# A four-branch graph network on one core: the sum carried from one tile of edges to the next leaves the products as a column and is added by VectorE, instead of being a row of the product's input

## The reference

```
edge_index = jnp.stack([src, dst])
h = jnp.maximum(_layernorm(x), 0.0);  x = x + gcn(h, edge_index, ...)     # 512 -> 128 -> 512
h = jnp.maximum(_layernorm(x), 0.0);  x = x + sage(h, src, dst, ...)      # three layers, below
h = jnp.maximum(_layernorm(x), 0.0);  x = x + edges(h, edge_index, ...)   # messages, below
h = jnp.maximum(_layernorm(x), 0.0);  x = x + last(h, edge_index, ...)    # mean, two products, batch norm

# sage, for l in range(3):
h_neigh = jax.ops.segment_sum(h[src], dst, num_segments=n) / deg
rst = jax.nn.relu(h @ W_self[l] + h_neigh @ W_neigh[l] + b[l])
h = rst / jnp.maximum(jnp.sqrt(jnp.sum(rst * rst, axis=-1, keepdims=True)), EPS)

# edges:
hidden = mish(concat([h[src], h[dst], edge_attr]) @ W1 + b1)
messages = mish(hidden @ W2 + b2)
agg = jax.ops.segment_sum(messages, dst, num_segments=n)
u = mish(concat([h, agg]) @ W3 + b3);  out = layernorm(h + u @ W4 + b4)
```

## Time and profile before

| | |
|---|---|
| timed, median of 3 runs | 3239.72 us (3235.13 to 3242.54) |
| the profiled execution's own time | 3228.05 us |
| its span | 3226.3 us |
| PE busy (matmuls) | 2661.2 us, 82% |
| DVE / ACT / POOL busy | 1783.5 / 1490.4 / 1351.1 us |
| mean granted clock of PE | 0.949 |
| SP's DMA queue | 359870 packets, 369.76 MB |

### The profile page before, as it was taken

The page is one execution under the profiler, slowest core; times in us unless marked ns, Lnnn a source line. Parts: engine busy times, 40 slices in busy tenths (PEclk is TensorE's granted clock), DMA queues, the critical chain, the costliest instruction groups (busy, mean ns, idle before and its releaser), DMA issues. The chain is left out here.

```text
span 3226.3 us, 47724 instructions
## 1 busy us (share of the span) xinstructions
PE 2661.2 (82%) x13893; PEld 1437.7 (45%) x13893; DVE 1783.5 (55%) x3993; ACT 1490.4 (46%) x2158; POOL 1351.1 (42%) x2421
## 2 busy tenths in 40 slices
PE   0025669778797999799996988979999999899976
PEld 0025533333343444344453545655555555444444
DVE  7625657656764874489764443425555556423234
ACT  3216746433432442245432774546666666432152
POOL 3664568858632332156543541113333333300136
PEclk9999988989999999999997998999999999999985
DMA  5418956646744784466644322222222233300148
GB/s 166 147 50 256 289 178 213 198 131 154 181 121 128 181 197 116 128 209 218 200 143 149 92 84 79 67 81 99 98 98 98 98 118 131 119 1 22 48 167 349
DMA packets 390005, 451.65 MB, mean 140 GB/s; under 512 B 202419, under 2 KB 228388, under 8 KB 387165
## 3 DMA queue, kind: packets, MB, share of 16 engines
q1 hardware_dynamic: 359870, 369.76, 37.0%
q0 software_dynamic: 29984, 80.02, 8.5%
HBM read 190.68 MB, written 217.75 MB: 127 GB/s over the span
## 5 line engine op out<-in xcount | busy, mean ns | idle before, releaser
L217 PE MATMUL s_ps_z<-s_w,slots 128*128 128x512 f16 x2844 | 647.8, 383 | 64.7 <-DMA s_bias<-in_L_gnn_b 43.1
L217 PEld LDWEIGHTS s_ps_z<-s_w,slots 128*128 128x128 f16 (+1 forms) x2844 | 277.7, 99 | 391.6 <-issue 48.2
L1352 ACT ACTIVATE s_g<-s_g,s_rn 128x512 f32<-128x512 f32 x237 | 170.3, 718 | 304.2 <-POOL s_rn L1231 304.0
L2019 PE MATMUL u_ps_o<-u_w,u_uT 128*128 128x512 f32 x632 | 288.5, 599 | 0.3 <-DVE u_uT L1890 0.3
L1281 DVE SCALAR_TENSOR_TENSOR s_g<-s_ps_z,s_f,s_bias 128x512 f32<-128x512 f32 x237 | 177.4, 748 | 195.2 <-PE s_ps_z L217 186.0
L1231 POOL TENSOR_TENSOR s_rn<-s_em,minus_half 128x1 f32<-128x1 f32 x237 | 171.9, 726 | 212.5 <-DVE s_em L1296 206.5
L2001 PE MATMUL u_ps_z<-slots,u_w 128*128 (+2 forms) x1920 | 236.1, 273 | 0.0
L2127 PE MATMUL z_ps_z<-slots,z_w 128*128 128x512 f16 (+1 forms) x960 | 210.1, 378 | 7.2 <-DMA z_w<-split_root 7.2
L2001 PEld LDWEIGHTS u_ps_z<-slots,u_w 128*128 128x128 f16 x1920 | 173.5, 98 | 37.5 <-issue 0.4
L707 DVE BATCH_NORM_STATS2 u_ny_st<-u_ps_o 128x6 f32<-128x512 f32 x79 | 54.7, 693 | 212.7 <-PE u_ps_o L2019 212.7
L734 ACT ACTIVATE u_h<-u_x,u_n_sh,u_n_rs 128x512 f32<-128x512 f32 x79 | 64.2, 813 | 229.2 <-POOL u_n_sh L729 229.2
(11 more groups left out here) (362 smaller groups left out, 5652.5 us busy)
## 6 DMA issues: line engine op xcount, KB each, us to landing
h_rows<-s_g SPq DMA_DIRECT2D x158, 256.0 KB, 2.3
x_rows<-r_x SPq DMA_DIRECT2D x79, 256.0 KB, 2.9
s_x<-x_rows SPq DMA_DIRECT2D x79, 256.0 KB, 2.9
x_rows<-s_x SPq DMA_DIRECT2D x79, 256.0 KB, 2.0
h_rows<-s_h SPq DMA_DIRECT2D x79, 256.0 KB, 2.4
u_x<-x_rows SPq DMA_DIRECT2D x79, 256.0 KB, 2.9
x_rows<-u_x SPq DMA_DIRECT2D x79, 256.0 KB, 2.1
h_rows<-u_h SPq DMA_DIRECT2D x79, 256.0 KB, 2.3
```

The lines of the kernel that those rows point to most:

```text
L217: ins = nc.tensor.matmul(out_ap, a(c), w[:, part * size + c * n:part * size + (c + 1) * n], start=first and c == 0 and m == 0, stop=stop a ...
L1352: nc.scalar.activation(g[b][:, :], g[b][:, :], ACT.Relu, scale=rn[v.buf(2)][:, 0:1]).then_inc(s_h, 1)
L2019: ins = nc.tensor.matmul(ps_o[b][:, :], ut_tile(v, c), w4[:, c * D:(c + 1) * D], start=False, stop=c == C - 1)
```

## The change

The carry's product and the carry row are gone. Columns of the selections `RAW` and `MEAN` that were for row 0 (column 0) now hold the selection of the carry, so the sums' own product gives, as column 0 of each feature chunk, what goes on to the next tile. Row 0 of `sl` is zero in SBUF, and only rows 1 to 127 are fetched. What row 0 of the selection did is done by VectorE in float32: row 0 is fetched a second time, spread to all 128 partitions (`w0`), and `total = w0 * on + ps_a` is formed for each chunk, where `on` is column 0 of the tile before. `total` is written over `m`, so `m` is free only when `lo` is done, not when the product is done. `hi` and `lo` read `total`, columns 1 to 127. `batch_rows` has one buffer for `sl` and `w0` (`nsel=1`). In `sage_layer` the unused output of `length` goes to PSUM (in `ps_c`'s place) as float32. In `prepare` PE makes the carry column three times. `unscale` is made in `node_update` by DVE.

```diff
+    class Carry:
+        def load(self, sp, t, kind):
+            b = t.buf(self.n)
+            wait_count(sp, self.s_added, t.t + 1 - self.n)
+            sp.dma_start(self.w0[b][:, :],
+                         sel_d[0:1, bass.ds(t.t * SELW + kind * P, P)].to_broadcast([P, P])).then_inc(self.w0_in[b], 16)
...
+        def add(self, dve, t, ps_a, total):
+            b, w0 = t.buf(2), t.buf(self.n)
+            dve.wait_ge(self.w0_in[w0], 16 * (t.uses(self.n) + 1))
+            wait_count(dve, self.s_on, t.t)
+            for c in range(C):
+                ins = nc.vector.scalar_tensor_tensor(out=total[:, c, :], in0=self.w0[w0][:, :],
+                                                     scalar=self.on[1 - b][:, c:c + 1], in1=ps_a[:, c * P:(c + 1) * P],
+                                                     op0=MUL, op1=ADD)
+            ins.then_inc(self.s_added, 1)
+            dve.wait_ge(self.s_added, t.t + 1)
+            nc.vector.tensor_copy(self.on[b][:, :], total[:, :, 0]).then_inc(self.s_on, 1)
...
         def load(self, sp, e):
-            wait_count(sp, self.s_sum, e.t - 1)
-            sp.dma_start(self.sl[e.buf(2)][:, :],
-                         sel_d[:, e.t * SELW + self.kind * P:e.t * SELW + (self.kind + 1) * P]).then_inc(
-                self.sel_in[e.buf(2)], 16)
+            b = e.buf(self.nsel)
...
+            wait_count(sp, self.s_sum, e.t + 1 - self.nsel)
+            sp.dma_start(self.sl[b][1:P, :],
+                         sel_d[1:P, e.t * SELW + self.kind * P:e.t * SELW + (self.kind + 1) * P]).then_inc(
+                self.sel_in[b], 16)
+            self.carry.load(sp, e, self.kind)
...
         def gather(self, pool, e):
             b = e.buf(self.nm)
-            wait_count(pool, self.s_sum, e.t + 1 - self.nm)
+            wait_count(pool, self.s_lo, e.t + 1 - self.nm)
...
         def sums(self, pe, e):
             b = e.buf(self.nm)
-            pe.wait_ge(self.s_carried, e.t + 1)
-            nc.tensor.matmul(self.ps_c[0:1, :], carry_c[:, e.t:e.t + 1], self.m[b][:, :], start=True,
-                             stop=True).then_inc(self.s_carry, 1)
...
-            wait_count(pe, self.s_lo, e.t)
...
+            wait_count(pe, self.carry.s_added, e.t)
             for c in range(C):
                 ins = nc.tensor.matmul(self.ps_a[:, c * P:(c + 1) * P], self.m[b][:, c * P:(c + 1) * P],
-                                       self.sl[e.buf(2)][:, :], start=True, stop=True)
+                                       self.sl[e.buf(self.nsel)][:, :], start=True, stop=True)
...
-                    pipeline(dve, NT, (FT - 2, edge_carry), (0, z_sum), (0, length), (0, clamp), (2, lo_rows),
+                    pipeline(dve, NT, (0, z_sum), (FT - 2, edge_add), (0, length), (0, clamp), (2, lo_rows),
                              (FT - 2, edge_lo), (FT - 3, edge_moments), edges=edges, loop_end=LOOP_END)
...
                     for c in range(C):
-                        if c < len(edges_of(g + 1)):
-                            sums.carry(dve, edges_of(g + 1)[c])
                         if 0 < c <= len(edges_of(g + 1)):
-                            sums.lo(dve, edges_of(g + 1)[c - 1])
+                            sums.add(dve, edges_of(g + 1)[c - 1])
                         dve.wait_ge(s_z, C * g + c + 1)
...
+                        if 0 < c <= len(edges_of(g + 1)):
+                            sums.lo(dve, edges_of(g + 1)[c - 1])
                     if len(edges_of(g + 1)) == C:
+                        sums.add(dve, edges_of(g + 1)[C - 1])
                         sums.lo(dve, edges_of(g + 1)[C - 1])
```

More of the change, by code:

```diff
@@ L185, in gnn_program @@
     floor_col = sb(top, "floor_col", [P, 1])
-    unscale = sb(top, "unscale", [P, P], F16)
     slots16 = slots[:, :].bitcast(F16)
@@ L1041, in __init__ @@
             self.m = [sb(ctx, f"{phase}_m{b}", [P, D]) for b in range(nm)]
[L1042 to L1045, removed]
+            self.sl = [sb(ctx, f"{phase}_sel{b}", [P, P]) for b in range(nsel)]
+            self.s_sum, self.s_hi, self.s_lo = sems(phase, "sum ahi alo")
@@ L1046, in __init__ @@
+            self.m_in, self.sel_in = pair(phase, "min", nm), pair(phase, "selin", nsel)
+            self.carry = Carry(ctx, f"{phase}_carry", nsel)
             self.norm = Norm(ctx, f"{phase}_en", 2) if normed else None
@@ L1148, in halves @@
                 return tuple(t[:, k * D:(k + 1) * D].rearrange("p (c n) -> p c n", c=C) for k in range(2))
-            sums = EdgeSums(ctx, phase, h_d[l] if l else x1_d, MEAN, scale_in, 2, halves, ps_a, ps_c, normed=l == 0)
+            sums = EdgeSums(ctx, phase, h_d[l] if l else x1_d, MEAN, scale_in, 2, halves, ps_a, normed=l == 0)
             s_inv, s_slot, s_slot_i = sems(phase, "inv slot sloti")
@@ L1159, in edge_gather, with edge_add @@
                 sums.gather(nc.gpsimd, e)
-            def edge_carry(e):
-                sums.carry(nc.vector, e)
+            def edge_add(e):
+                sums.add(nc.vector, e)
             def edge_lo(e):
@@ L1270, in _ @@
                 dve.wait_ge(s_f, 1)
+                sums.clear(nc.vector, *(t[:, :] for t in aT))
                 dve.wait_ge(s_w, 32)
@@ L1637, in _ @@
                 dve.wait_ge(s_f, 1)
+                passed.clear(dve, *(t[0:1, :] for t in sl), *(t[:, :] for t in aT))
                 def z_sum(v):
@@ L1647, in cap, with add @@
                     mish.cap(dve, r[:, :], v, s_sum, v.t - 1)
-                def carry(v):
-                    dve.wait_ge(mish.s_u, v.t + 1)
-                    if isinstance(v.t, int) and v.t == 0:
-                        nc.vector.memset(mish.c[v.buf(2)][0:1, :], 0.0).then_inc(s_carried, 1)
-                        return
-                    dve.wait_ge(s_carry, v.t)
-                    nc.vector.tensor_copy(mish.c[v.buf(2)][0:1, :], ps_c[0:1, :]).then_inc(s_carried, 1)
+                def add(v):
+                    dve.wait_ge(s_sum, v.t + 1)
+                    wait_count(dve, s_aT, v.t)
+                    passed.add(dve, v, ps_a[v.buf(2)], total[:, :].rearrange("p (c n) -> p c n", c=C))
                 def totals(v):
@@ L1753, in node_update @@
             minus_f = sb(ctx, "u_minus_f", [P, 1])
+            unscale = sb(ctx, "u_unscale", [P, P], F16)
             uT = [sb(ctx, f"u_uT{b}", [P, C * 2 * P]) for b in range(2)]
@@ L1867, in _ @@
                 dve.wait_ge(s_w, 96)
+                nc.vector.tensor_scalar(out=unscale[:, :], in0=ident[:, :], scalar1=1.0 / SCALE_LN, scalar2=None, op0=MUL)
                 nc.vector.tensor_scalar(out=w4[:, :], in0=w4[:, :], scalar1=f[:, 0:1], scalar2=None,
@@ L2085, in _ @@
                                         scalar2=None, op0=MUL).then_inc(s_f, 1)
+                sums.clear(dve, *(t[:, :] for t in aT))
                 for g in range(GROUPS):
```

102 lines of the change are left out of this document (57 added, 45 removed).

## The result

The changed kernel takes 3409.39 us (median of 4 runs, 3405.21 to 3413.42), the one before, run beside it, 3241.13: a ratio of 1.0522 (1.0501 to 1.0542), +168 us. The prediction said slower, 3364 (3300 to 3415): the direction and the range hold, and the loss is 44 us larger than its +124. The profiled execution took 3405.21, its span is 3403.2.

A forecast was written before the change was run, and what follows sets the result against it. PE was taken to bound layer 0, `edge_messages` and `batch_rows`. Terms 58.9 + 79.8 + 17.5 − 8 − 16.4 − 8.6 + 1 = +124.2 us on the profiled 3228.05 gave 3352.3, on the median 3364 (3300 to 3415).

The forecast's parts named there:

- The loop: Layers 0 and 1: adds awaiting sums delay the next `sl` fetch; steps 10.3 and 11.4 us, +58.9 and +79.8.
- S+5.27: Layers 0 and 1: the next `sl` fetch is issued 5.27 us after S, the start of a tile's sums.
- The 127 rows: Fetch of `sl`: 127 rows go through one DMA engine, 2.8 us more on the landing.
- The clock: Layers 0 and 1: idle PE drops its clock, half of 38 sums take 0.92 us longer, +17.5.
- Layer 2: Layer 2: `sl` landing, 7.1 us against 6.4 in hand, eats most of PE's 0.95 a step; −8 us.
- batch_rows: `batch_rows`: −19 us from PE, +5.8 at group boundaries, +4.6 in the last group; together −8.6.
- edge_messages: `edge_messages`: bound by PE, −19 us, less two open tails of adds at 1.3 each; −16.4.
- the PE term of 0.95 a step: Carry products gone from PE: −0.95 us x 20 in each zone that PE bounds.
- Rival 1: Fetch of 127 rows spreads over 16 engines, landings stay 2.2 and 3.3 us: 3208 to 3228, say 3222; chance 0.13.
- Rival 2: The second fetch, `w0`, comes last; each us late costs 38, so 3402 for one; chance 0.06.
- The PSUM term (+1): `length` output to PSUM: +1 us, bounds 0 to 14.

The follow-up runs named there:

- experiment 5: Changed kernel with 13 (layer 0) or 18 (layer 1) unread PE products ahead of each sums: 3358.61 us against 3220.55 for the kernel before.
- experiment 3: Changed kernel with VectorE's adds moved behind `lo_rows`, 127 rows kept: 3270.3 us against 3241.03 for the kernel before.
- experiment 4: Changed kernel with the two fetches first in SyncE's list, 127 rows and early adds kept: 3193.28 us against 3241.03 for the kernel before.
- experiment 1: Kernel before with only rows 1 to 127 of `sl` fetched, nothing else moved: 3277.88 us against 3241.03.
- experiment 2: Changed kernel with `sl` fetched as 128 rows and `w0` in its own DRAM tensor: 3255.21 us against 3241.03 for the kernel before.
- experiment 9: Changed kernel with only 122 rows of `sl` fetched (6 to 127): 3279.1 us against 3221.85 for the kernel before.
- experiment 6: Changed kernel with the two fetches first in SyncE's list and layer 0's moments ahead of `lo`: 3184.56 us against 3220.55 for the kernel before.
- experiment 8: Changed kernel with 128 rows, fetches first in SyncE's list and layer 0's moments behind the adds: 3149.41 us against 3220.55 for the kernel before.

## Why the prediction was right, and where its sizes were off

*The loop* is shown, link by link, and it is what the forecast of +124 rests on. At the full clock the changed kernel issues the fetch at S+5.27 (the two full-clock steps of layer 0, and the median of 30 steps of experiment 5): the prediction's figure to the hundredth, which is part luck, since single links were off by up to 0.06 and cancelled. At the low clock it is S+6.19, the 0.92 more of the sums. Experiments 3 and 4 cut the loop at two different links, and both take away most of the loss.

*The 127 rows* are shown by experiments 1, 2 and 9. The term was 2.8 us; with and without, the landings differ by at least 3.2 in layer 0 and by 2.8 in layer 1. But I had added it to medians of the kernel before: 5.0 and 6.1 became 5.49 and 6.57, 0.5 more in each of 38 steps, 18 us.

*The clock* was, for its size, mis-sized most. I let half of the 38 sums be low, because a low step leaves less idle. In the changed kernel 15 of 20 were in layer 0 and all 20 in layer 1. Over the 38 steps the issue of the fetch came 29.4 us later than S+5.27 would give, not 17.5: 12 of the missing 44. What failed was "that step's idle is only 2 to 3 us, and the next may run at full clock". The idle behind a low step had a median of 3.3 us in layer 0 and 4.1 in layer 1. And 2 to 3 us did not keep the clock up either: idles of 2.5 (experiment 2) and 2.2 (experiment 5) were followed by low sums. Experiment 5, with 6 low sums of 40, brings the 29.4 down to 7.

*The first fetch of a zone* had no term in the sum. PE already waited for it in layer 1 of before (5.13 idle), so a longer landing counts in full. From the start of a layer's projection to its first sums it took 3.9 and 3.2 us more in layers 0 and 1, and +0.5 and −0.9 in experiment 2 with its 128 rows. That is 7 us. The tails of the two zones, where the last adds lie open, are another 4. With the 18 and the 12 these make 41 of the 44; what is left lies within the differences of the other stages.

*Layer 2* came out near (−11 for −8) by a wrong mechanism, that is by luck. I had `sl` late; it is the gather that is late, landing in 6.8 instead of 4.9 beside the 127 rows. With 128 rows it lands in 4.6 and the step is 6.5.

*`batch_rows`*: −3.9 for −8.6. There too the sums wait for the gather, 0.3 to 0.8 us in 8 of 20 tiles. It may now go out only after `lo`, since the totals are written over `m`; the prediction named that wait for layer 0 alone. With 128 rows the stage takes 296, so 8 of the 12 us that it could win are lost to the row count. `edge_messages` (−18.6 for −16.4) and the PE term of 0.95 a step held: its mean step fell from 9.01 to 8.06.

*The rivals.* Rival 1 (the rows spread) is refuted as a fact, but as a sum it was sound in direction only: with 128 rows the kernel is 14 us slower, not 19 faster, since the low clock and `w0` reach into that case: its "PE's idle of 2 us leaves the clock up" failed in ten steps of layer 1, where the sums were low after idles of 2.0 to 2.8 us. Rival 2 is seen only in experiment 2, where the adds wait for `w0` in 16 steps of layer 0 at some 0.34 each; in the changed kernel `sl` itself is later.

Left open: the 5.6 us ahead of layer 0, which lie within what that part shows between runs (681.8 to 696.8 in the thirteen profiles), and why `finish` has two lengths. The PSUM term (+1) was not tried by itself.

## What to carry to other kernels

Before counting what a change takes from the busiest engine, follow from the new wait to the next instance of itself: an instruction that waits for this step's result and stands ahead of the issue of the next step's input turns a hidden landing time into step time. When a tile loses a row, look at how many DMA engines the new count gives: here 127 rows instead of 128 were worth 154 us, and one name moved in SyncE's list 216. And once PE waits in every step, price its clock too: here 35 of 40 sums were low, not half of them.

## What the runs showed of the hardware that was not expected

- A fetch on one DMA engine slows its neighbours. In layer 2 the gather's landing went from 4.9 to 6.8 us, and from 4.9 to 5.8 by the row count alone (experiment 1). In layer 0 it is 5.4 us with 127 rows and 3.7 with 128 (experiments 6 and 8), worth 26 us though `sl` itself was hidden. The place counts too: with the fetch first in SyncE's list the gather of layer 2 lands in 4.4 even beside 127 rows (experiment 4).
- The fetch that is issued behind it takes longer to issue: that of `w0` took a median of 0.98 us in layers 0 and 1 and 2.4 in layer 2, against 0.44 and 0.45 when `sl` had 128 rows.
- The granted clock fell to 0.50 after idles of 2.0 to 2.8 us that came back in every step (layer 1 of experiment 2), but not after each: one sums there ran at the full clock after 3.05 us.
- The same last stage took 113 or 126 to 130 us, whatever the kernel; over most of it the DMA engines moved 388 GB/s in the profile of before and 337 in that of the changed kernel.
